# The first chunks of a perceiver block: who writes the warm-up's tile, and where the query work stands

## The chip, the cores and the metric

The kernel runs on one core of a Trainium2 chip. The metric is the device time of one execution in microseconds (us); lower is better. The engines are TensorE (PE; its weight loads are PEld), VectorE (DVE), ScalarE (ACT), GpSimd (POOL) and SyncE (SP), which here issues most of the DMA transfers. Each engine works through its own instructions in order, and semaphores order them among each other.

## The reference

x is 256 tokens of 512 values, the context is 4096 tokens of 512. Three residual steps follow each other. What this case touches is the first of them, cross-attention with 16 heads of 32:

```python
q = _qdq(x) @ _qdq(wq).T + bq          # x after layernorm
kv = cond @ wkv.T + bkv
k, v = jnp.split(kv, 2, axis=-1)
attn = jax.nn.softmax(jnp.einsum('bnhd,bmhd->bhnm', q, k) * scale, axis=-1)
o = jnp.einsum('bhnm,bmhd->bnhd', attn, v).reshape(B, N, C)
out = _qdq(o) @ _qdq(wp).T + bp
```

_qdq rounds to 8-bit steps with one scale for each token or each output channel. After it come a causal self-attention (16 query heads of 128, 4 key heads) and a feed-forward with silu(gate) * up, each after a layernorm and each added to x.

## The kernel before

The context is worked through in eight chunks of 512 tokens. For each chunk c PE computes four key blocks (`key_block`, 12 matmuls of 128x512 each: high and low parts of both operands, three passes over four slices) and four value tiles (12 matmuls each). ScalarE rounds the chunk's data to a high part (`high`, into h_ring), VectorE computes the low part (`low`, l_ring). ScalarE evacuates keys to kh_buf, VectorE computes their rest (`k_low`, kl_buf), and SyncE stores both to DRAM scratch, from where heads are loaded later into k_stack. Chunks 0 and 1 are written out; the rest run in a loop over pairs, the last pair written out again.

Chunk 0 is special: its data and the key weights come in four pieces, and PE works piece by piece (lines L1331 to L1337). Ahead of it, `keep_busy(7, 7)` issues seven fp32 matmuls of ident with itself (L1242), once GpSimd has written ones, ident and ident_b.

The query work is threaded into chunk 1. VectorE normalizes x, quantizes it to in_q (`quantize_tokens`), and quantizes wq and wp in halves (`quantize_weight_half`, nth 0 and 1 for wq, 2 and 3 for wp; each ends in w_q, L917, and counts w_used). Into these it threads `k_low` of chunk 1 and `low` of chunk 2. PE does `prepare_queries` between the keys and values of chunk 1: a row of token scales (ones times diag, L1262), the transposes of in_q (L396), then those of wq (L1254, after w_used 2). Ahead of value tile 3 it transposes wp; after tile 3, `project_queries` makes the row of wp's scales (L1280) and 16 projections (L1287). ScalarE copies the results to in_t, wq_t, wp_t (L662), sx_row and swp_row. VectorE then runs `split_queries`: high and low parts of the queries, which SyncE stores and loads again as q_max and q_stack (`load_q`). From chunk 2 on, PE threads first products of queries and keys (L1295) behind value tiles; they need q_max and k_stack.

The tile q_f lies in diag, k_stack[0] lies over the tiles of the query preparation, and bp_row over swp_row. PSUM has eight banks; `bank(i)` is one of them.

Of the kernel before, what the change touches and what calls it, by code (L numbers as in the profile page):

```python
# [109 lines left out]
def perceiver(nc, x_in, stream, wq_in, wp_in, bias_cols, bias_rows, out):  # L110
    with ExitStack() as ctx:
# [122 lines left out]
        q_f = diag[:, 0:NT, :].rearrange("p t n -> p (t n)")  # L234
# [18 lines left out]
        consts_ready = sem("consts_ready")  # L253
# [169 lines left out]
        def _(sp):  # L423
# [65 lines left out]
            sp.wait_ge(q_stored, 32 * KT)  # L489
            load_q(q_max[0], qm_loaded[0], 0)  # L490
# [65 lines left out]
        def _(pool):  # L556
# [12 lines left out]
            nc.gpsimd.memset(ones[:], 1.0).then_inc(consts_ready, 1)  # L569
# [7 lines left out]
            pool.wait_ge(ql_ready, KT)  # L577
            pool.wait_ge(ones_set, 1)
# [53 lines left out]
        def _(act):  # L632
# [32 lines left out]
            def context_chunk(i, k):  # L665
                c = 2 * i + k
                first, second = (isinstance(i, int) and c == n for n in range(2))
                if not first:
                    act.wait_ge(v_done, 4 * c)
                    high(act, c + 3, 1 - k, i + 1)  # L670
                for g in range(KT):
                    act.wait_ge(k_done, 4 * c + g + 1)
                    wait(act, k_stored[g], 32 * c)
                    nc.scalar.activation(kh_buf[:, g, :], key_bank(c, g), ACT.Identity,  # L674
                                         bias=biases[:, KT + g:KT + g + 1]).then_inc(kh_evac, 1)
                if first:
                    high(act, CTX0 + 1, 1, 1)
                if second:
                    act.wait_ge(row_done, 1)
                    nc.scalar.copy(sx_row[:], bank(5)[:, 0:N]).then_inc(row_evac, 1)  # L680
                    evacuate_tokens(0, in_t)
                    evacuate_transposed(3, (6, 7), wq_t)
                for mt in range(4):
                    if second and mt == 3:
                        evacuate_transposed(4, (4, 5), wp_t)
                    act.wait_ge(v_done, 4 * c + mt + 1)
                    nc.scalar.copy(v_all[:, :, 4 * c + mt, :],  # L687
                                   value_bank(c, mt).rearrange("p (h d) -> p h d", d=DH)).then_inc(v_evac, 1)
                if second:
                    act.wait_ge(row_done, 2)  # L690
                    nc.scalar.copy(swp_row[:], bank(6)).then_inc(row_evac, 1)

            context_chunk(0, 0)
            context_chunk(0, 1)
            with act.Fori(1, NCTX // 2) as i:
                context_chunk(i, 0)
                context_chunk(i, 1)
# [196 lines left out]
        def _(dve):  # L894
            order = Order(dve, dve_order)
            for kt in range(KT):
                dve.wait_ge(piece_loaded[kt], 32)
                nc.vector.tensor_copy(wkv_h[0][:, kt, :], wkv_raw[:, 0, kt, :]).then_inc(piece_wh, 1)
                dve.wait_ge(piece_wh, kt + 1)
                nc.vector.tensor_tensor(wkv_l[0][:, kt, :], wkv_raw[:, 0, kt, :], wkv_h[0][:, kt, :].bitcast(F32),  # L900
                                        ALU.subtract).then_inc(piece_l if kt < KT - 1 else l_ready, 1)
                wait_piece(dve, kt, piece_h, h_ready, 1)
                nc.vector.tensor_tensor(l_ring[0][:, kt, :], f_ring[0][:, kt, :], h_ring[0][:, kt, :].bitcast(F32),
                                        ALU.subtract).then_inc(piece_l if kt < KT - 1 else l_ready, 1)
# [15 lines left out]
            def token_row():  # L920
                dve.wait_ge(consts_ready, 3)
# [10 lines left out]
            def split_queries():  # L932
                dve.wait_ge(row_evac, 2)
                for g in range(KT):
# [3 lines left out]
                        out=q_f, in0=bank(7 if g < 2 else 4)[:, at], scalar=wq_s[:, g:g + 1], in1=sx_row[:],  # L938
# [30 lines left out]
            low(dve, CTX0 + 2, 0)  # L969
            quantize_weight_half(1, wq_s, between=lambda: k_low(1, 2))  # L970
            k_low(1, 3)
            for nth in (2, 3):
                quantize_weight_half(nth, wp_s)
# [261 lines left out]
        def _(pe):  # L1235
# [23 lines left out]
            def prepare_queries():  # L1259
# [4 lines left out]
                for t in range(NT):  # L1264
                    pe.wait_ge(quant_ready, t + 1)
                    transpose_tokens(t, in_q).then_inc(tr_done, 1)
                pe.wait_ge(w_used, 2)
                transpose_weights(0, (6, 7)).then_inc(tr_done, 1)

            def transpose_wp():  # L1270

                pe.wait_ge(w_used, 4)
                pe.wait_ge(tr_evac, 4)
# [3 lines left out]
            def project_queries():  # L1277

                pe.wait_ge(diag_ready, KT + NT)
                nc.tensor.matmul(bank(6), ones[:], diag[:].rearrange("p a n -> p (a n)"), start=True,  # L1280
                                 stop=True).then_inc(row_done, 1)
                for g in range(KT):
                    if g == 2:
                        pe.wait_ge(tr_evac, 6)
                    to = bank(7 if g < 2 else 4)[:, (g % 2) * N:(g % 2 + 1) * N]
# [3 lines left out]
                    if g % 2 == 1:  # L1289
                        last.then_inc(q_done, 1)  # L1290

# [25 lines left out]
            def context_chunk(i, k):  # L1317
# [35 lines left out]
                for mt in range(4):  # L1353
                    if second and mt == 3:
                        transpose_wp()
# [7 lines left out]
                    if k == 0 and not first:  # L1363
                        if mt == 0:
                            pe.wait_ge(qm_loaded[0], 48)
                            pe.wait_ge(k0_loaded, 48 * i)
                            pe.wait_ge(ql_ready, KT)

# [9 lines left out]
                if second:  # L1378
                    project_queries()

            pe.wait_ge(consts_ready, 3)
            keep_busy(7, 7)
# [404 lines left out]
```

## Time and profile before

| | |
|---|---|
| median of 3 runs | 617.87 us (616.87 to 618.75) |
| the profiled execution, its time | 621.24 us |
| its span, first to last instruction | 619.4 us |
| mean granted clock of TensorE | 0.994 |
| busy: PE, DVE, ACT, POOL | 597.2, 370.8, 302.9, 226.6 us |

A timeline row gives the start, the duration, the engine, the line of the kernel, the operation, the tile written and those read, the shapes and the count, and in brackets how long the engine sat idle before and what ended that. Matmuls are pipelined: the duration of one is longer than the distance to the next. A merged row (x16) has one duration from first start to last end.

### The profile page before, as it was taken

How to read it: one execution, taken by the hardware profiler on the slowest of the kernel's cores; microseconds unless marked ns; L12 is line 12 of the kernel's file. 1: busy time of each engine (PE TensorE's matmuls, PEld its weight loads, DVE VectorE, ACT ScalarE, POOL GpSimd, SP SyncE). 2: the span in 40 equal slices, each digit the busy share in tenths (PEclk: the TensorE clock that was granted, in tenths of full speed). 3: DMA queues.
4: the chain of work that ended last, by engine and by line, in shares of the span. 5: the costliest groups of instructions: out<-in, count | busy, mean ns of one | idle time of the engine just before them, and what ended most of it. 6: DMA issues, size and time to landing. Idle time of an engine off the chain costs nothing.

```text
span 619.4 us, 12489 instructions
## 1 busy us (share of the span) xinstructions
PE 597.2 (96%) x4386; PEld 478.7 (77%) x4386; DVE 370.8 (60%) x688; ACT 302.9 (49%) x437; POOL 226.6 (37%) x111
## 2 busy tenths in 40 slices
PE   8989999999999999999999999999799899999997
PEld 6867788888887667667777667775698789799996
DVE  4796622331434778787888788876754244376562
ACT  3444232333232666665566656555248668644441
POOL 0000200000002778888878888881001554410000
PEclk9999999999999999999999999999999899999999
DMA  8765456525629655566665556610041425245410
GB/s 292 277 215 167 164 181 195 176 95 162 210 95 274 185 155 152 149 159 164 163 158 148 148 153 167 161 57 2 1 146 58 138 72 200 69 181 194 174 63 34
DMA packets 29902, 92.19 MB, mean 149 GB/s; under 512 B 5488, under 2 KB 9584, under 8 KB 23280
## 3 DMA queue, kind: packets, MB, share of 16 engines
q1 hardware_dynamic: 28624, 89.67, 47.3%
q10 hardware_dynamic: 1248, 2.10, 0.9%
q8 instruction: 20, 0.33, 0.2%
q14 instruction: 10, 0.08, 0.0%
HBM read 65.02 MB, written 18.35 MB: 135 GB/s over the span
## 4 chain that ended last, share of the span: by engine, by line
PE 82%; DVE 9%; ACT 4%; issue 2%; POOL 2%; DMA 1%; SPq 0%; POOLq 0%; ACTq 0%; DVEq 0%
PE ps L341 15%; PE ps L342 14%; PE ps L343 14%; PE ps L1313 11%; PE ps L1420 9%; PE ps L1432 9%; PE ps L1446 4%; POOL p_sum L592 1%; PE ps L1409 1%; DVE kl_buf L950 1%; ACT h_ring L795 1%; DMA k_stack<-kh_scratch 1%; PE ps L1331 1%; DVE l_ring L314 1%; DMA f_ring<-stream 1%
## 5 line engine op out<-in xcount | busy, mean ns | idle before, releaser
L991 DVE TENSOR_REDUCE m_part<-ps 128x1 f32<-128x512 f32 x240 | 150.4, 683 | 39.4 <-PE ps L1313 39.1
L718 ACT ACTIVATE p_ring<-ps 128x1024 f32<-128x1024 f32 x128 | 125.8, 1023 | 80.0 <-PE ps L1420 44.2
L592 POOL TENSOR_TENSOR p_sum<-p_sum,p_ring 128x1024 f32<-128x1024 f32 x60 | 142.7, 2378 | 9.0 <-ACT p_ring L718 4.8
L1313 PE MATMUL ps<-k_stack,q_max 96*128 96x512 f32 x240 | 85.6, 427 | 1.5 <-issue 0.8
L1420 PE MATMUL ps<-q_stack,k_stack 98*128 98x256 f32 x512 | 80.7, 285 | 0.1
L1420 PEld LDWEIGHTS ps<-q_stack,k_stack 98*128 98x128 f32 x512 | 74.6, 189 | 6.8 <-ACT p_ring L718 1.7
L1432 PE MATMUL ps<-p_ring,v_head 128*32 128x256 f32 x1024 | 71.6, 383 | 0.1
L1313 PEld LDWEIGHTS ps<-k_stack,q_max 96*128 96x128 f32 x240 | 40.8, 188 | 26.4 <-issue 15.1
L950 DVE SCALAR_TENSOR_TENSOR kl_buf<-ps,biases,kh_buf 128x512 fp32r<-128x512 f32 x32 | 23.7, 749 | 58.2 <-ACT kh_buf L674 57.8
L314 DVE TENSOR_TENSOR l_ring<-f_ring,h_ring 128x2048 fp32r<-128x2048 f32 x22 | 50.2, 2288 | 12.5 <-ACT h_ring L310 12.5
L341 PE MATMUL ps<-xt_h,h_ring 128*128 128x256 f32 x200 | 56.8, 284 | 0.0
L343 PE MATMUL ps<-xt_h,l_ring 128*128 128x256 f32 x200 | 56.6, 283 | 0.0
L342 PE MATMUL ps<-xt_l,h_ring 128*128 128x256 f32 x200 | 56.6, 283 | 0.0
L687 ACT COPY v_all<-ps 128x512 f32 (+1 forms) x32 | 18.8, 588 | 68.2 <-PE ps L343 68.2
L592 POOL TENSOR_TENSOR p_sum<-p_ring 128x1024 f32<-128x1024 f32 x15 | 35.9, 2391 | 42.2 <-ACT p_ring L718 42.2
L1432 PEld LDWEIGHTS ps<-p_ring,v_head 128*32 128x32 f32 x1024 | 31.4, 109 | 25.2 <-issue 8.2
L341 PE MATMUL ps<-wkv_h,h_ring 128*128 128x512 f32 x128 | 50.9, 397 | 0.0
L342 PE MATMUL ps<-wkv_l,h_ring 128*128 128x512 f32 x128 | 50.4, 394 | 0.0
L343 PE MATMUL ps<-wkv_h,l_ring 128*128 128x512 f32 x128 | 50.4, 393 | 0.0
L310 ACT CAST h_ring<-f_ring 128x2048 fp32r<-128x2048 f32 x23 | 43.9, 1908 | 7.2 <-PE ps L343 7.2
L674 ACT ACTIVATE kh_buf<-ps,biases 128x512 fp32r<-128x512 f32 x32 | 21.7, 690 | 50.7 <-PE ps L343 47.8
L619 POOL TENSOR_TENSOR l_ring<-f_ring,h_ring 128x2048 fp32r<-128x2048 f32 x7 | 32.2, 4594 | 37.3 <-ACT h_ring L795 28.9
(197 smaller groups left out, 1087.8 us busy)
## 6 DMA issues: line engine op xcount, KB each, us to landing
f_ring<-stream SPq DMA_DIRECT2D x29, 1024.0 KB, 5.0
k_stack<-kh_scratch SPq DMA_DIRECT2D x60, 256.0 KB, 4.5
kh_scratch<-kh_buf SPq DMA_DIRECT2D x32, 256.0 KB, 4.8
kl_scratch<-kl_buf SPq DMA_DIRECT2D x32, 256.0 KB, 5.5
v_head<-v_all SPq DMA_DIRECT2D x16, 512.0 KB, 3.0
k_stack<-kl_scratch SPq DMA_DIRECT2D x30, 256.0 KB, 4.1
v_all<-stream SPq DMA_DIRECT2D x4, 256.0 KB, 4.7
f_ring<-stream SPq DMA_DIRECT2D x4, 256.0 KB, 5.7
```

Source lines behind the costliest of these rows:

```text
L310: nc.scalar.copy(h_ring[which][:], f_ring[which][:]).then_inc(h_ready, 1)
L314: nc.vector.tensor_tensor(l_ring[which][:], f_ring[which][:], h_ring[which][:].bitcast(F32), ALU.subtract).then_inc(l_ready, 1)
L341: nc.tensor.matmul(out_ap, lh, rh, start=start, stop=False)
L342: nc.tensor.matmul(out_ap, lh, rl, start=False, stop=False)
L343: return nc.tensor.matmul(out_ap, ll, rh, start=False, stop=stop)
L592: nc.gpsimd.tensor_tensor(p_sum[:, p, :], p_ring[:, 0, :] if n == 0 else p_sum[:, p, :], p_ring[:, c % 4, :], ALU.add).then_inc(sums_done, 1)
L619: nc.gpsimd.tensor_tensor(l_ring[w][:], f_ring[w][:], h_ring[w][:].bitcast(F32), ALU.subtract).then_inc(l_ready, 1)
L718: nc.scalar.activation(p_ring[:, c % 4, :], ps[:, 2 * (c % 2):2 * (c % 2) + 2, :].rearrange("p b n -> p (b n)"), ACT.Exp, scale=XSCALE).th ...
L991: nc.vector.reduce_max(m_part[:, j // NT, j % NT:j % NT + 1], maximum_bank(j), AX.X).then_inc(max_read, 1)
L1313: nc.tensor.matmul(maximum_bank(j), q_max[p][0:SPLIT_ROWS, at128(j % NT)], k_stack[p][0:SPLIT_ROWS, j // NT * D:(j // NT + 1) * D], start= ...
L1420: last = nc.tensor.matmul(ps[:, 2 * (c % 2) + k // 2, (k % 2) * N:(k % 2 + 1) * N], k_stack[p][0:SPLIT_ROWS + MAX_ROWS, at128(4 * c + k)], ...
L1432: last = nc.tensor.matmul(bank(7)[k * DH:(k + 1) * DH, 0:N], v_head[p][:, 4 * c + k, :], p_ring[:, c % 4, k * N:(k + 1) * N], start=c == 0 ...
```

## The change

VectorE writes ones at its start, with a semaphore of its own (ones_ready); PE warms up with eleven fp32 matmuls of ones with itself as soon as that is there, and waits for GpSimd's two ident tiles behind them. The transposes of wq move from ahead of value tile 0 of chunk 1 to ahead of value tile 1; those of wp move from ahead of tile 3 to behind the projections, which come right after tile 3; the row of wp's scales comes last, into bank 2. q_f moves into in_q, the queries' banks are 6 and 7. VectorE's low of chunk 2 moves behind the second half of wq and k_low(1, 3). ScalarE does high of chunk 3 at the end of chunk 1 rather than at the start of chunk 2, and its chunks 2 and 3 are written out. SyncE, GpSimd and PE wait for the second row copy (row_evac 2) ahead of their first use of what lies over the preparation's tiles.

```diff
--- before.py
+++ after.py
@@ -231,7 +231,7 @@
         wkv_raw = v_all[:].rearrange("p h m d -> p (h m d)")[:, 0:2 * KT * D].rearrange(
             "p (w k n) -> p w k n", w=2, k=KT)
         bp_row = swp_row
-        q_f = diag[:, 0:NT, :].rearrange("p t n -> p (t n)")
+        q_f = in_q[:].rearrange("p t d -> p (t d)").bitcast(F32)[:, 0:N]
 
         qh_buf = x_hat[:].rearrange("p t (g n) -> p (t g) n", n=N)
         ql_buf = o_all[:].rearrange("p t (g n) -> p (t g) n", n=N)
@@ -250,7 +250,7 @@
         x_loaded, rows_loaded, w_loaded = sem("x_loaded"), sem("rows_loaded"), [sem("w_loaded0"), sem("w_loaded1")]
         biases_loaded = sem("biases_loaded")
         w_used = sem("w_used")
-        consts_ready = sem("consts_ready")
+        consts_ready, ones_ready = sem("consts_ready"), sem("ones_ready")
         pool_order, dve_order = sem("pool_order"), sem("dve_order")
         dve_order_b, dve_order_c = sem("dve_order_b"), sem("dve_order_c")
         var_ready, rstd_ready = sem("var_ready"), sem("rstd_ready")
@@ -487,6 +487,7 @@
             context_chunk(0, 1)
             store_q()
             sp.wait_ge(q_stored, 32 * KT)
+            sp.wait_ge(row_evac, 2)
             load_q(q_max[0], qm_loaded[0], 0)
             load_q(q_stack[0], qs_loaded[0], 0)
             with sp.Fori(1, NCTX // 2 - 1) as i:
@@ -566,7 +567,6 @@
             order.step(nc.gpsimd.memset(minus_half[:], -0.5))
             for tile in (ident, ident_b):
                 order.step(nc.gpsimd.memset(tile[:], 0.0))
-            nc.gpsimd.memset(ones[:], 1.0).then_inc(consts_ready, 1)
             for tile in (ident, ident_b):
                 nc.gpsimd.affine_select(out=tile[:], in_=tile[:], compare_op=ALU.not_equal, fill=1.0, base=0,
                                         pattern=[[-1, P]], channel_multiplier=1).then_inc(consts_ready, 1)
@@ -575,6 +575,7 @@
 
 
             pool.wait_ge(ql_ready, KT)
+            pool.wait_ge(row_evac, 2)
             pool.wait_ge(ones_set, 1)
             nc.gpsimd.memset(k_stack[0][SPLIT_ROWS:P, :].bitcast(F32), 1.0).then_inc(ones_set, 1)
             pool.wait_ge(k_done, KT * NCTX)
@@ -664,8 +665,8 @@
 
             def context_chunk(i, k):
                 c = 2 * i + k
-                first, second = (isinstance(i, int) and c == n for n in range(2))
-                if not first:
+                first, second, third = (isinstance(i, int) and c == n for n in range(3))
+                if not first and not third:
                     act.wait_ge(v_done, 4 * c)
                     high(act, c + 3, 1 - k, i + 1)
                 for g in range(KT):
@@ -679,20 +680,22 @@
                     act.wait_ge(row_done, 1)
                     nc.scalar.copy(sx_row[:], bank(5)[:, 0:N]).then_inc(row_evac, 1)
                     evacuate_tokens(0, in_t)
-                    evacuate_transposed(3, (6, 7), wq_t)
                 for mt in range(4):
-                    if second and mt == 3:
-                        evacuate_transposed(4, (4, 5), wp_t)
+                    if second and mt == 1:
+                        evacuate_transposed(3, (6, 7), wq_t)
                     act.wait_ge(v_done, 4 * c + mt + 1)
                     nc.scalar.copy(v_all[:, :, 4 * c + mt, :],
                                    value_bank(c, mt).rearrange("p (h d) -> p h d", d=DH)).then_inc(v_evac, 1)
                 if second:
+                    high(act, CTX0 + 3, 1, 2)
+                    evacuate_transposed(4, (4, 5), wp_t)
                     act.wait_ge(row_done, 2)
-                    nc.scalar.copy(swp_row[:], bank(6)).then_inc(row_evac, 1)
-
-            context_chunk(0, 0)
-            context_chunk(0, 1)
-            with act.Fori(1, NCTX // 2) as i:
+                    nc.scalar.copy(swp_row[:], bank(2)).then_inc(row_evac, 1)
+
+            for i in range(2):
+                context_chunk(i, 0)
+                context_chunk(i, 1)
+            with act.Fori(2, NCTX // 2) as i:
                 context_chunk(i, 0)
                 context_chunk(i, 1)
 
@@ -893,6 +896,7 @@
         @block.vector
         def _(dve):
             order = Order(dve, dve_order)
+            nc.vector.memset(ones[:], 1.0).then_inc(ones_ready, 1)
             for kt in range(KT):
                 dve.wait_ge(piece_loaded[kt], 32)
                 nc.vector.tensor_copy(wkv_h[0][:, kt, :], wkv_raw[:, 0, kt, :]).then_inc(piece_wh, 1)
@@ -918,7 +922,7 @@
                 dve.wait_ge(w_used, nth + 1)
 
             def token_row():
-                dve.wait_ge(consts_ready, 3)
+                dve.wait_ge(consts_ready, 2)
                 for t in range(NT):
                     nc.vector.tensor_scalar(diag[:, t, :], ident[:], tok_s[:, t:t + 1], None,
                                             ALU.mult).then_inc(diag_ready, 1)
@@ -930,12 +934,12 @@
                                             ALU.mult).then_inc(diag_ready, 1)
 
             def split_queries():
-                dve.wait_ge(row_evac, 2)
+                dve.wait_ge(row_evac, 1)
                 for g in range(KT):
                     dve.wait_ge(q_done, g // 2 + 1)
                     at = slice((g % 2) * N, (g % 2 + 1) * N)
                     order.step(nc.vector.scalar_tensor_tensor(
-                        out=q_f, in0=bank(7 if g < 2 else 4)[:, at], scalar=wq_s[:, g:g + 1], in1=sx_row[:],
+                        out=q_f, in0=bank(6 + g // 2)[:, at], scalar=wq_s[:, g:g + 1], in1=sx_row[:],
                         op0=ALU.mult, op1=ALU.mult))
                     nc.vector.tensor_scalar(qh_buf[:, g, :].bitcast(F32R), q_f, biases[:, g:g + 1], None,
                                             ALU.add).then_inc(qh_ready, 1)
@@ -966,9 +970,9 @@
             quantize_weight_half(0, wq_s, between=lambda: k_low(1, 0))
             token_row()
             k_low(1, 1)
-            low(dve, CTX0 + 2, 0)
             quantize_weight_half(1, wq_s, between=lambda: k_low(1, 2))
             k_low(1, 3)
+            low(dve, CTX0 + 2, 0)
             for nth in (2, 3):
                 quantize_weight_half(nth, wp_s)
             dve.wait_ge(rows_loaded, 32)
@@ -1264,30 +1268,35 @@
                 for t in range(NT):
                     pe.wait_ge(quant_ready, t + 1)
                     transpose_tokens(t, in_q).then_inc(tr_done, 1)
+
+            def transpose_wq():
+
                 pe.wait_ge(w_used, 2)
                 transpose_weights(0, (6, 7)).then_inc(tr_done, 1)
 
             def transpose_wp():
 
                 pe.wait_ge(w_used, 4)
-                pe.wait_ge(tr_evac, 4)
                 pe.wait_ge(row_evac, 1)
                 transpose_weights(1, (4, 5)).then_inc(tr_done, 1)
 
             def project_queries():
 
-                pe.wait_ge(diag_ready, KT + NT)
-                nc.tensor.matmul(bank(6), ones[:], diag[:].rearrange("p a n -> p (a n)"), start=True,
-                                 stop=True).then_inc(row_done, 1)
+                pe.wait_ge(tr_evac, 4)
                 for g in range(KT):
-                    if g == 2:
-                        pe.wait_ge(tr_evac, 6)
-                    to = bank(7 if g < 2 else 4)[:, (g % 2) * N:(g % 2 + 1) * N]
+                    to = bank(6 + g // 2)[:, (g % 2) * N:(g % 2 + 1) * N]
                     for kt in range(KT):
                         last = nc.tensor.matmul(to, wq_t[:, kt, at128(g)], in_t[:, kt, :], start=kt == 0,
                                                 stop=kt == KT - 1)
                     if g % 2 == 1:
                         last.then_inc(q_done, 1)
+
+            def weight_row():
+
+                pe.wait_ge(v_evac, 7)
+                pe.wait_ge(diag_ready, KT + NT)
+                nc.tensor.matmul(bank(2), ones[:], diag[:].rearrange("p a n -> p (a n)"), start=True,
+                                 stop=True).then_inc(row_done, 1)
 
             def first_maximum_tile(j, k_at, read):
 
@@ -1351,8 +1360,10 @@
                     pe.wait_ge(v_evac, 4)
                     prepare_queries()
                 for mt in range(4):
-                    if second and mt == 3:
-                        transpose_wp()
+                    if second and mt == 1:
+                        transpose_wq()
+                    if k == 0 and not first and mt == 0:
+                        pe.wait_ge(row_evac, 2)
                     wait(pe, v_evac, 4 * c + mt - 1)
                     for kt in range(KT):
                         if first and mt == 0 and kt == KT // 2:
@@ -1365,6 +1376,7 @@
                             pe.wait_ge(qm_loaded[0], 48)
                             pe.wait_ge(k0_loaded, 48 * i)
                             pe.wait_ge(ql_ready, KT)
+                            pe.wait_ge(tr_evac, 6)
 
                         first_maximum_tile(mt, bass.ts(2 * i - 2 + mt // NT, D), 0 if mt < 2 else 4 * i - 5 + mt)
                     if last_one and mt in (1, 2):
@@ -1377,9 +1389,13 @@
                     pe.wait_ge(max_read, 4 * i)
                 if second:
                     project_queries()
-
-            pe.wait_ge(consts_ready, 3)
-            keep_busy(7, 7)
+                    transpose_wp()
+                    weight_row()
+
+            pe.wait_ge(ones_ready, 1)
+            for _ in range(11):
+                nc.tensor.matmul(bank(7)[:, 0:P], ones[:], ones[:], start=True, stop=True)
+            pe.wait_ge(consts_ready, 2)
             context_chunk(0, 0)
             context_chunk(0, 1)
             with nc.tensor.Fori(1, NCTX // 2 - 1) as i:
```

## Rows read from the trace of the kernel before

**Rows 1.** The page, part 1: busy us, share, instructions.
```profile
PE 597.2 (96%) x4386; PEld 478.7 (77%) x4386; DVE 370.8 (60%) x688; ACT 302.9 (49%) x437; POOL 226.6 (37%) x111
```

**Rows 2.** Windows, PE: stretch and length, busy (instructions), granted clock, DMA share, GB/s.
```profile
100.00:124.00 24.00, 24.00 (x108) 1.00 0.54 182
11.00:12.00 1.00, 1.00 (x4) 1.00 1.04 426
46.00:47.00 1.00, 1.00 (x6) 0.50 0.79 158
```

**Rows 3.** Timeline of PE, start: start us, us, what, count [idle before].
```profile
2.26 3.35 PE L1242 MATMUL ps<-ident 128*128 128x128 f32 x14 [2.26 <-POOL ident_b L571]
6.16 2.04 PE L1331 MATMUL ps<-h_ring,wkv_h 128*128 128x512 f32 x4 [0.55 <-ACT h_ring L635]
8.01 0.63 PE L1335 MATMUL ps<-h_ring,wkv_l 128*128 128x512 f32 x1
...
11.42 1.26 PE L1331 MATMUL ps<-h_ring,wkv_h 128*128 128x512 f32 x4
12.52 0.39 PE L1335 MATMUL ps<-h_ring,wkv_l 128*128 128x512 f32 x1
12.75 0.40 PE L1337 MATMUL ps<-l_ring,wkv_h 128*128 128x512 f32 x1
```

**Rows 4.** Timeline of PE, 45 to 77 us.
```profile
45.12 1.19 PE L1254 MATMUL ps<-ident_b,w_q 128*128 128x128 bf16 x16 [2.54 <-DVE w_q L917]
46.07 0.78 PE L341 MATMUL ps<-wkv_h,h_ring 128*128 128x512 f32 x1
...
49.73 0.40 PE L341 MATMUL ps<-wkv_h,h_ring 128*128 128x512 f32 x1
...
59.62 1.02 PE L1280 MATMUL ps<-diag,ones 128*128 128x512 f32 x2
60.48 1.91 PE L1287 MATMUL ps<-in_t,wq_t 128*128 128x256 bf16 x16
62.14 0.48 PE L341 MATMUL ps<-h_ring,wkv_h 128*128 128x512 f32 x1
...
68.35 0.50 PE L341 MATMUL ps<-h_ring,wkv_h 128*128 128x512 f32 x1 [0.49 <-DVE kl_buf L950]
...
76.65 0.40 PE L1295 MATMUL ps<-k_stack,q_max 96*128 x1
```

**Rows 5.** Timeline of VectorE (DVE), 14 to 67 us.
```profile
14.80 2.36 DVE L907 TENSOR_TENSOR wkv_l<-v_all,wkv_h 128x1024 fp32r<-128x1024 f32 x2 [2.13 <-ACT wkv_h L649]
19.50 2.73 DVE L950 SCALAR_TENSOR_TENSOR kl_buf<-ps,biases,kh_buf 128x512 fp32r<-128x512 f32 x4 [2.33 <-ACT kh_buf L674]
...
38.09 2.28 DVE L314 TENSOR_TENSOR l_ring<-f_ring,h_ring 128x2048 fp32r<-128x2048 f32 x1
...
44.37 0.69 DVE L917 TENSOR_SCALAR w_q<-w_raw 128x1024 bf16<-128x1024 f32 x1
...
55.53 0.87 DVE L929 TENSOR_SCALAR diag<-ident,wp_s 128x128 f32<-128x128 f32 x4
...
66.81 0.48 DVE L943 SCALAR_TENSOR_TENSOR o_all<-diag,biases,x_hat 128x256 fp32r<-128x256 f32 x1
```

**Rows 6.** Timeline of all engines, first 2 us.
```profile
0.75 1.28 ACT L635 ACT_TABLE_LOAD   x1 [0.75 <-PEq L1780]
...
1.42 0.20 POOL L569 MEMSET ones<- 128x128 f32 x1
```

**Rows 7.** DMA issues of 11.0 to 11.5 us: queue, count, KB, us to landing.
```profile
x_cur<-x_in ACTq DMA_DIRECT2D x1, 512.0 KB, 6.5
```

**Rows 8.** Timeline of ScalarE (ACT), near 57 us.
```profile
57.00 1.93 ACT L662 COPY wp_t<-ps 128x1024 bf16<-128x1024 bf16 x2 [0.32 <-PE ps L1254]
```

**Rows 9.** Timeline of SyncE's DMA queue (SPq), near 73 us.
```profile
73.41 0.32 SPq L462 DMA_DIRECT2D k_stack<-kh_scratch  x1
```

**Rows 10.** DMA issues of 72.0 to 73.8 us.
```profile
k_stack<-kl_scratch SPq DMA_DIRECT2D x1, 128.0 KB, 2.8
```

## The prediction

> **What bounds the kernel now.** I read the page first. TensorE (PE) is busy for 597.2 of the 619.4 us [rows 1], and the page's chain that ended last is mostly PE's. So a microsecond taken from PE ahead of the chunk loop ends in the total, if nothing else sets the pace of that loop. The windows of the steady chunks show PE busy for all 24.00 us of 24.00 [rows 2]: the loop is PE's own work, and what comes before it is shifted as a block. The change lies ahead of 62 us, so I read only that part closely.
>
> Next came PE's waits up to 70 us, where the one for w_q is the longest, and then PE's timeline, which shows three places where PE loses time.
>
> First place, the start. The warm-up runs from 2.26 us, after GpSimd's ident_b, to 5.61; the first real matmul starts at 6.16 [rows 3]. The eight 128x512 matmuls from 8.01 to 11.42 start 0.427 us apart. At 12.52 and 12.75 they are 0.23 us apart [rows 3]. The four matmuls between 11.42 and 12.52 take 1.10 us, which fits one at the old distance and three at the new, so PE's clock doubled at about 11.85 us. The column of the granted clock reads 1.00 here [rows 2]; it seems to hold nothing before its first change, and the distances decide: 1.2 GHz before, 2.4 GHz after.
>
> Second place, the query weights. PE finishes the tokens' transposes at 42.59 and waits 2.54 us for w_q, until 45.12 [rows 4]. Then the granted clock is down to 0.50 [rows 2]. From 46.07 to 49.73 there are nine distances, 3.66 us; at 0.227 us each they are 2.04; the later distances are short again from about 49.35. The fall costs 1.6 us on top of the wait.
>
> Third place, chunk 2. It starts at 62.14, and its third key block waits 0.49 us for kl_buf [rows 4]; with the restart, 0.88 us from matmul to matmul in place of 0.23, so 0.65 lost. VectorE was held by split_queries until 67.29 [rows 5].
>
> **Change, first part: the warm-up.** It removes GpSimd's memset of ones and PE's wait for three constants, and gives the memset to VectorE, which has nothing to do before the first piece of data. The engines' first instructions start at 0.75 [rows 6]. The trace has no VectorE memset. Bounds: 0.1 us (nothing but issue) and 0.5 us; GpSimd's memset of this very tile takes 0.20 [rows 6], which I take. PE starts at about 1.0 in place of 2.26. Seven fp32 matmuls are 14 records in 3.35 us, 0.21 apart but for the first, so eleven are 22 records, about 4.8 us, ending near 5.9 with the slow clock and earlier with the fast one. The first real matmul waits for h_ring's first piece as now, so it stays at 6.16; if the memset took 0.5 us, it would be late by about 0.1.
>
> What is gained is the moment at which the clock rises. The only other rise, at 49.35, came 4.2 us after PE resumed at 45.12 [rows 4]. The first came 5.7 us after the resumption at 6.16, and 9.6 after the first warm-up matmul. With PE running from 1.0 without the gap, 4.2 to 5.7 us give a rise at 5.2 to 6.7. Every matmul between the rise and 11.85 costs 0.227 in place of 0.427: with a rise at or before 6.16 that is 5.69 x 0.47 = 2.7 us, less some 0.1, an estimate, for l_ring's first piece, which PE then wants as soon as VectorE has it. With a rise at 6.7 it is 2.3. Supply should not take it back: the next piece is there when PE comes to it by the timeline of both engines, and ScalarE begins its next copy only after the last piece. Bounds: nothing (the rise stays where it is) and 2.6. I take 2.3.
>
> The Trainium skill's page "TensorE: Matmul & The Clock Gate", in Part 1 on the HAM clock gate, says that what watches PE's activity runs free of the kernel's start, so that the number of slow matmuls differs from run to run. The rows above are one execution and cannot show this. By that rule the first term would be a different one in each run, on either side of 2.3; by the rows it would be 2.3 each time. I use this for a rival below.
>
> Does the rest follow? VectorE's wkv_l halves end at 17.16 whatever PE does, and k_low(0, ...) starts at 19.50 now [rows 5]. So VectorE moves 2.34 us ahead, nearly as much as PE. x_cur, issued before 11.5 and 6.5 us on the way [rows 7], has landed by 18.0, ahead of its use at 19.8. f_ring's next chunk is wanted 2.3 us earlier as well; I assume it there, and its low has 2.4 us to spare. ScalarE's copies follow PE. The tightest place is k_low(1,0), due at 33.3, with PE's third key block of chunk 1 at 33.5: no wait, or 0.2.
>
> **Second part: wq behind value tile 0, low of chunk 2 behind k_low(1,3).** PE goes from the tokens' transposes (about 40.0) straight to value tile 0, 12 matmuls, 2.7 us, to 42.7. VectorE has w_q's second half at 45.06 now [rows 5]. It starts 2.34 earlier, and the 2.28 us of low(CTX0 + 2) no longer stand ahead of it [rows 5]: 40.5. So the transposes at 42.7 have 2.2 us to spare, the 2.54 us of waiting disappear, and with them the reason for the clock's fall. What covers the stall is the value tile; were it gone (the weights over 2.2 us late), each further microsecond would be on PE again. The low that is moved ends at 43.4 and is wanted by chunk 2 at 55: 12 us to spare. The load and the two pairs of K stores that SyncE holds behind it start near 43.4, ahead of today's, which come after w_q at 45.06. ScalarE's wq_t copies now stand between value copies 0 and 1; PE asks for copy 0 only at tile 2.
>
> The wait is worth 2.5. The fall is worth 1.6 in this execution, nothing in one where it does not happen. The three timed runs lie 1.9 us apart (616.87 to 618.75), as wide as this term, so I do not count it whole: 1.2.
>
> **Third part: queries ahead of wp's transposes, weight row last.** The same 16 projections (1.66 us), 16 transposes (0.95) and two records of the row (0.86) are issued [rows 4], in another order; nothing is saved on PE. VectorE's diag of wp_s ends at 56.40 now [rows 5], 54.06 after the shift. PE projects from about 52.0 to 53.6, transposes wp to 54.6 and then asks for diag: 0.5 us to spare. Chunk 2 starts at 55.5. split_queries no longer waits for swp_row, its 5.7 us run from 54.1 to 59.8, and k_low(2,0) is there at 60.6 or 60.8; PE wants it at 60.9. So the 0.65 us go, or all but 0.2. I take 0.6.
>
> ScalarE gets high(CTX0 + 3), 1.9 us, ahead of the wp_t copies, 1.93 [rows 8], and swp_row: 52.6 to about 57.2, with the first key block of chunk 2 ready at 58.3. Two more unrolled chunks on ScalarE add no work. SyncE's new wait for swp_row (57.2) stands ahead of load_q, and behind it are the K loads and chunk 2's K stores; it already waits there for q_stored, which comes after the last split at 59.8, so it costs nothing. GpSimd's k_stack memset likewise. PE's new waits ask for things long done.
>
> **The sum.** 2.3 + 2.5 + 1.2 + 0.6 = 6.6 us. Of this execution alone it would be 2.5 + 2.5 + 1.6 + 0.65 = 7.3: a span of 612.1 in place of 619.4, and a time of 613.9 in place of 621.24. The profiled time is 3.4 us above the median shown, so I take the sum from the median: 617.87 - 6.6 = 611.3.
>
> **Rivals.**
> (a) The clock decides otherwise: the rise does not come earlier, or not in most runs, and the fall was seldom there. Left are 2.5 + 0.6 and a part of the rest, 3.1 to 5: 612.9 to 614.8. For it: the rise in the start came late although PE had been at work since 2.26. Against: the gap from 5.61 to 6.16 goes. The skill's rule above points this way for single runs.
> (b) The stall moves: PE waits for wq or for diag, because VectorE, which works without a break up to 56.40, is later than the shift says. The slack at diag is 0.5 us; with 2 to 3 us late, 4 to 5 are left of the 6.6: 613 to 614.
> (c) The change comes to nothing: all of it is taken back before the loop ends, for instance by a fixed transfer. PE's 24.00 of 24.00 busy speaks against it. 617.9.
> (d) Slower: SyncE's wait for swp_row. Behind it stand load_q and load_k0. Today the last quarter of k_stack is issued at 73.41, 6.1 us after split_queries ends, and lands 2.8 us later at most, at 76.2 [rows 9, 10]; PE asks at 76.65 [rows 4], 14.5 us into chunk 2. In the new order that is 68.7 against 70.0, 1.3 us of slack, and swp_row comes 2.6 us ahead of the last split. So PE waits only when swp_row is over 3.9 us late, and past 3.9 + 6.6 = 10.5 us late the kernel is slower; 13 us late gives 620.4. Nothing in ScalarE's load speaks for it.
>
> **Chances.** Forecast, with its own range 609.3 to 612.8: 0.62. (a) 0.20, (b) 0.10, (c) 0.04, (d) 0.04. The range must leave out no more than 2 in 10: from 609.3 (both clock terms whole and the median run of before in the unlucky state) to 614.6. What can be told from no change is 0.3%, 1.9 us. Faster 0.92, same 0.04, slower 0.04.
>
> **What would show it.** PE's first matmul at about 1.0 us, waiting for VectorE; matmuls 0.23 apart from 6 or 7 us on; no wait for w_q, and no slice of granted clock under 1.00 near 45 us; wq's transposes at about 43, chunk 2's first matmul near 55.5; no wait for kl_buf in chunk 2. It would be wrong by the first term if the distances stay 0.427 until 10 us or later, by the second if PE stands before the wq transposes, and by the third if it stands before the weight row.

## The result, and the profile after

The changed kernel takes 614.99 us (median of five, 614.48 to 616.02), against 618.75 (616.87 to 619.93) for five runs of the kernel before. The ratio is 0.9946, interval 0.9925 to 0.9968: 3.3 us off, where I forecast 6.6 and a ratio of 0.9893. (The ratio compares fast executions alone, and is not the quotient of the two medians, 0.9939; of all executions below, the one of 856.25 us in run 10, at a mean granted clock of 0.635, is left out as slow.) The kernel is faster, and 0.4 us outside the range of 609.3 to 614.6. The median of before had been 617.87 over three runs; this makes 0.9 us of the miss of 3.7.

The profiled execution of the changed kernel has a span of 614.2 us and a time of 616.02, that is 5.2 us less than the profiled execution of before. The page, part 1, which answers to [rows 1]:

```profile
PE 596.1 (97%) x4394; PEld 478.5 (78%) x4394; DVE 370.9 (60%) x689; ACT 302.8 (49%) x437; POOL 226.4 (37%) x110
```

The timeline of PE in the first chunks, which answers to [rows 3, 4]:

```profile
1.06 5.06 PE L1397 MATMUL ps<-ones 128*128 128x128 f32 x22 [1.06 <-DVE ones L899]
5.89 1.45 PE L1340 MATMUL ps<-h_ring,wkv_h 128*128 128x512 f32 x4
7.18 0.39 PE L1344 MATMUL ps<-h_ring,wkv_l 128*128 128x512 f32 x1
7.40 0.39 PE L1346 MATMUL ps<-l_ring,wkv_h 128*128 128x512 f32 x1
```

```profile
42.62 1.07 PE L1258 MATMUL ps<-ident_b,w_q 128*128 128x128 bf16 x16
43.50 0.47 PE L341 MATMUL ps<-wkv_h,h_ring 128*128 128x512 f32 x1
...
51.79 1.92 PE L1289 MATMUL ps<-in_t,wq_t 128*128 128x256 bf16 x16
53.55 1.06 PE L1258 MATMUL ps<-ident_b,w_q 128*128 128x128 bf16 x16
54.44 1.08 PE L1298 MATMUL ps<-diag,ones 128*128 128x512 f32 x2
54.96 0.79 PE L341 MATMUL ps<-h_ring,wkv_h 128*128 128x512 f32 x1
```

The warm-up starts at 1.06, after VectorE's ones, and runs into the first real matmul without a gap. From 7.18 on the distances (from one start to the next) are 0.22 us. wq's transposes come at 42.62 without idle time (42.7 forecast). The projections, wp's transposes and the weight row follow each other, and chunk 2 starts at 54.96 (55.5 forecast). PE's waits of the first 100 us are now one row:

```profile
PE ps L1397 <- DVE ones L899: 1.1, 1, 1.1
```

VectorE has the second half of w_q at 40.26 (40.5), the weight row's diag at 53.82 (54.06), and its first k_low of chunk 2 at 60.41 (60.6). This answers to [rows 5]:

```profile
39.57 0.69 DVE L921 TENSOR_SCALAR w_q<-w_raw 128x1024 bf16<-128x1024 f32 x1
...
40.97 2.28 DVE L314 TENSOR_TENSOR l_ring<-f_ring,h_ring 128x2048 fp32r<-128x2048 f32 x1
...
52.94 0.88 DVE L933 TENSOR_SCALAR diag<-ident,wp_s 128x128 f32<-128x128 f32 x4
...
59.66 0.75 DVE L954 SCALAR_TENSOR_TENSOR kl_buf<-ps,biases,kh_buf 128x512 fp32r<-128x512 f32 x1 [0.26 <-DVE o_all L947]
```

ScalarE's copy to swp_row ends at 57.07, and SyncE goes on to load_q at 61.16. So up to chunk 2 every row stands within 0.6 us of where the prediction put it, and the two profiles are 7.7 us apart there (7.3 forecast for this pair): ScalarE's first value copy of chunk 2 is at 69.20, against 76.95. Where the other 2.5 us of this pair went, the windows of PE show (stretch and length, busy, granted clock, DMA share, GB/s):

```profile
44.00:45.00 1.00, 1.00 (x6) 1.00 1.00 156
428.00:429.00 1.00, 0.53 (x7) 1.00 0.00 0
429.00:430.00 1.00, 0.58 (x7) 0.87 0.00 0
430.00:431.00 1.00, 1.00 (x8) 0.50 0.08 16
431.00:432.00 1.00, 1.00 (x4) 0.50 0.00 0
432.00:433.00 1.00, 1.00 (x4) 0.50 0.00 0
433.00:434.00 1.00, 1.00 (x7) 0.92 0.00 0
```

The clock stays up near 45 us, as forecast, but falls from 1.00 to 0.50 at 429.7 (from here on, a fall), in a stage that the change doesn't touch: PE idles there, for 1.52 and 0.42 us, while VectorE quantizes the attention's output. In the profile of before the same two gaps bring no fall. It costs 1.5 us (from out_t's copy to xt_h's, 11.29 us against 9.78). The rest is 0.7 in the attention's heads and 0.3 at their beginning.

But 5.2 us is one pair of executions, and the medians are 3.8 apart. The question is thus which of the terms were the change's, and which belonged to the one execution of before that I had read.

### The profile page after: what moved, and what is told of

It is laid out like the page before. It is cut to its first block, busy times and chain, and to the rows that moved or that the text cites. A ratio compares the mean times of both kernels' runs of the same rounds, so it can differ in the third digit from the quotient of the medians.

```text
span 614.2 us, 12490 instructions
## 1 busy us (share of the span) xinstructions
PE 596.1 (97%) x4394; PEld 478.5 (78%) x4394; DVE 370.9 (60%) x689; ACT 302.8 (49%) x437; POOL 226.4 (37%) x110
## 4 chain that ended last, share of the span: by engine, by line
PE 88%; DVE 4%; ACT 3%; issue 2%; POOL 1%; DMA 1%; POOLq 0%; SPq 0%; ACTq 0%; DVEq 0%
PE ps L341 16%; PE ps L342 16%; PE ps L343 16%; PE ps L1322 11%; PE ps L1436 9%; PE ps L1448 9%; PE ps L1462 4%; POOL p_sum L593 1%; PE ps L1425 1%; ACT h_ring L798 1%; PE ps L1397 1%; DMA k_stack<-kh_scratch 1%; PE ps L1340 1%; PE ps L1304 1%; DVE p_sum L1075 1%
## 5 line engine op out<-in xcount | busy, mean ns | idle before, releaser
L341 PE MATMUL ps<-xt_h,h_ring 128*128 128x256 f32 x200 | 56.8, 284 | 0.0
L687 ACT COPY v_all<-ps 128x512 f32<-128x512 f32 (+1 forms) x32 | 18.8, 589 | 67.4 <-PE ps L343 67.4
L583 POOL MEMSET k_stack<- 32x4096 f32 x1 | 3.5, 3522 | 115.4 <-PE ps L343 115.4
```

The source lines that it names most:

```text
L341: nc.tensor.matmul(out_ap, lh, rh, start=start, stop=False)
```

## The experiments

Two theories stood at first. A: the front gives what its two profiles show, in every execution, and a fall that the change brings about behind it takes a part back. B: the clock decides anew in each execution, and the profile of before was an unlucky one, in its start or near 45 us. The kernels ran four at a time on one chip (1 to 4, 5 to 8, 9 to 12), each four beside their own runs of the kernel before (32, 18 and 34), and each ratio is against those.

**1. The kernel before, again.** No edit.

> The kernel before once more, to see which of its clock falls are its own. Theory A (the front gives its 7.5 us in every run, and a fall that the change makes near 430 us takes 1.3 back): this profile has its fall near 46 us again, chunk 2 starts at 62.1, ratio 1.000. Theory B (which gap of PE brings a fall is decided anew in each execution, so the fall near 46 us was in the profile of before and not in most timed runs): the slow stretches lie elsewhere, chunk 2 starts at 60.5 without one near 46, and the ratio is 1.000 with the single runs 1.5 us or more apart.

Ratio 0.9999 (0.9979 to 1.0018). Its profile has a span of 614.9 us, not 619.4. Chunk 2 starts at 58.24: theory B had 60.5, without the fall, and the other 2.3 us are the start. The start, PE's timeline:

```profile
2.26 3.36 PE L1242 MATMUL ps<-ident 128*128 128x128 f32 x14 [2.26 <-POOL ident_b L571]
5.79 1.71 PE L1331 MATMUL ps<-h_ring,wkv_h 128*128 128x512 f32 x4 [0.17 <-ACT h_ring L635]
7.34 0.39 PE L1335 MATMUL ps<-h_ring,wkv_l 128*128 128x512 f32 x1
7.57 0.39 PE L1337 MATMUL ps<-l_ring,wkv_h 128*128 128x512 f32 x1
```

With the old warm-up and with a gap, the distances are down to 0.23 at 7.34. The four matmuls ahead of it take 1.55 us, so the clock rose near 7.1 us, not at 11.85. (The kept trace also records the moment of the clock's changes: 6.99 us here, 11.79 in the profile of before.) The gap ahead of the first real matmul doesn't explain the late rise: in run 4 it is 0.50 us, against 0.55 there, and the clock rises at 7.28. PE waits 2.68 us for w_q here, and the windows show no fall:

```profile
41.00:42.00 1.00, 0.00 (x0) 1.00 0.04 8
42.00:43.00 1.00, 0.18 (x3) 1.00 0.00 0
43.00:44.00 1.00, 1.00 (x17) 1.00 0.07 20
44.00:45.00 1.00, 1.00 (x6) 1.00 1.00 336
```

So two of my four terms rested on something that another execution of the same kernel doesn't have.

**2. The warm-up alone.** The memset of ones and the eleven matmuls in the kernel before:

```diff
-            pe.wait_ge(consts_ready, 3)
-            keep_busy(7, 7)
+            pe.wait_ge(ones_ready, 1)
+            for _ in range(11):
+                nc.tensor.matmul(bank(7)[:, 0:P], ones[:], ones[:], start=True, stop=True)
+            pe.wait_ge(consts_ready, 2)
```

> The warm-up alone: ones by VectorE, eleven matmuls of it, nothing else changed. Theory A: chunk 2 starts 2.6 us earlier, 59.5 with the fall near 46 us, ratio 0.996. Theory B: chunk 2 starts 2.6 us earlier in a profile with an early rise; on average 1.5 to 2.3 us, ratio 0.9965.

Ratio 1.0003 (0.9982 to 1.0024): nothing, where the theories expected 0.996 and 0.9965. PE's start is earlier in the profile (first key copy at 15.63, against 16.22 in 1), and VectorE's w_q comes earlier with it (second half at 42.41, against 42.77). But the wait for w_q is still there, 2.75 us, and this time with a fall:

```profile
40.00:41.00 1.00, 0.00 (x0) 1.00 0.00 0
41.00:42.00 1.00, 0.00 (x0) 1.00 0.03 8
42.00:43.00 1.00, 0.54 (x6) 0.53 0.00 0
43.00:44.00 1.00, 1.00 (x12) 0.50 0.41 41
44.00:45.00 1.00, 1.00 (x6) 0.50 1.04 406
45.00:46.00 1.00, 1.00 (x5) 0.77 0.96 283
```

**3. The order alone.** The changed kernel with GpSimd's ones and `keep_busy(7, 7)` as before.

> The order alone: seven matmuls of ident as before, everything else as changed. Theory A: 4.7 us off, ratio 0.992, less 1.3 where a fall follows near 430 us. Theory B: the wait's 2.5 us and kl_buf's 0.65 are left, the fall's 1.6 only now and then: 3.2 us, ratio 0.995.

Ratio 0.9932 (0.9909 to 0.9955). The order has the whole gain, within the intervals. Theory B's 0.995 lies inside the interval, and so does A's 0.992.

**4. The old order with the wait filled**, by ten more matmuls of ident that nobody reads (a filler).

```diff
+                keep_busy(10, 7)
                 pe.wait_ge(w_used, 2)
                 transpose_weights(0, (6, 7)).then_inc(tr_done, 1)
```

> The kernel before with ten fp32 matmuls of ident (some 2.3 us) issued by PE where it waits for wq's second half; the wait itself stays. Both: no fall near 46 us. Theory A: ratio 0.9974 (1.6 us off). Theory B: the fall was in a part of the runs only, ratio 0.998 to 1.000.

Ratio 0.9978 (0.9960 to 0.9996). PE still waits for w_q, 0.3 us behind the filler, and the clock stays up. This is 1.4 us for the falls at this place, with an interval of 0.2 to 2.5, which holds the values of both theories; the profile can't say how often they come.

**5 and 6. The changed kernel and the order alone, on one chip.** No new edit.

> The changed kernel once more, beside the order alone on one chip. Theory C (what the runs so far suggest: the clock of the kernel before rises near 6 to 7 us too in most executions, so that the longer warm-up has little to give, and the order alone carries the gain): ratio 0.993 to 0.995, within 0.2% of the order alone; matmuls 0.23 apart from 6 to 7 us on. Rival D (the warm-up gives 1 us or more): ratio under 0.9915 and under that of the order alone.

> The order alone, with the warm-up of the kernel before, again. Theory C: ratio 0.9935 with its first look repeated, chunk 2 near 55 us. Rival D: 0.994 or more, 1 us or more above the changed kernel.

0.9944 (0.9927 to 0.9961) and 0.9958 (0.9941 to 0.9974). The changed kernel is 0.14% ahead here; in the first comparisons it was 0.14% behind. The two differences cancel. Rival D wanted under 0.9915 for the changed kernel, which its interval excludes; the 0.9 us between the two here comes near D's 1 us, but in the first comparisons the sign is the other way.

**7. No warm-up at all.**

```diff
             pe.wait_ge(ones_ready, 1)
-            for _ in range(11):
-                nc.tensor.matmul(bank(7)[:, 0:P], ones[:], ones[:], start=True, stop=True)
             pe.wait_ge(consts_ready, 2)
```

> The changed kernel with no warm-up matmul at all: what the warm-up is worth. PE then starts with its first real matmul near 5.2 us and the clock rises 4 to 6 us later, 9.5 to 11. That is 3 to 4.5 us of matmuls at 0.427 in place of 0.227, 1.4 to 2.1 us, if the rest follows; where VectorE's own start sets the pace of chunk 1, less: ratio 0.996 to 0.998. If it is as fast as the changed kernel, the start isn't on the path at all.

Ratio 1.0015 (0.9988 to 1.0041): 4.4 us slower than the changed kernel, more than expected. PE's timeline, start:

```profile
5.85 2.05 PE L1340 MATMUL ps<-h_ring,wkv_h 128*128 128x512 f32 x4 [5.85 <-ACT h_ring L636]
7.70 0.63 PE L1344 MATMUL ps<-h_ring,wkv_l 128*128 128x512 f32 x1
8.12 0.63 PE L1346 MATMUL ps<-l_ring,wkv_h 128*128 128x512 f32 x1
...
11.85 0.39 PE L1344 MATMUL ps<-h_ring,wkv_l 128*128 128x512 f32 x1
12.09 0.40 PE L1346 MATMUL ps<-l_ring,wkv_h 128*128 128x512 f32 x1
```

The clock rises near 10.7 us, and the first key copy is at 18.03, 2 us late, as worked out. The rest of this profile's loss is elsewhere: at the end of the chunk loop PE stands 2.40 us, with no releaser shown, and then the clock is down for over six more:

```profile
194.54 0.80 PE L1322 MATMUL ps<-k_stack,q_max 96*128 96x512 f32 x2 [2.40 <-issue]
```

```profile
194.00:195.00 1.00, 0.46 (x2) 1.00 0.98 218
195.00:196.00 1.00, 1.00 (x6) 0.50 1.04 221
196.00:197.00 1.00, 1.00 (x4) 0.50 1.00 201
200.00:201.00 1.00, 1.00 (x4) 0.50 0.16 50
```

So a warm-up is worth something; it is the step from seven matmuls that end at 5.6 us to eleven that end near 5.9 that gives little. What PE stands for at the loop's end is a load of k_stack, as shown further down; why PE is so far ahead of it here stays open.

**8. The changed kernel with a longer filler at the output's quantization**, where the fall at 429.7 was:

```diff
-                keep_busy(2 if t else 10, 3)
+                keep_busy(2 if t else 15, 3)
```

> The changed kernel with five more fp32 matmuls of ident (15 in place of 10) in PE's gap at the quantization of the attention's output, where the profile of the changed kernel has its fall at 430 us. Both theories: no slow stretch between 425 and 440 us, 0.5 us off on average (1.3 us in the executions that had the fall): ratio 0.992 to 0.994, slow stretch near 478 us unchanged.

Ratio 0.9927 (0.9909 to 0.9946), 1.0 us under the changed kernel beside it, though the two intervals overlap, and no fall there:

```profile
428.00:429.00 1.00, 0.60 (x8) 1.00 0.00 0
429.00:430.00 1.00, 0.58 (x8) 1.00 0.00 0
430.00:431.00 1.00, 0.95 (x9) 1.00 0.06 16
431.00:432.00 1.00, 1.00 (x7) 1.00 0.00 0
```

That alone doesn't show that the filler prevents a fall: of the nine profiles without it only that of the changed kernel has one at this place; the other eight, run 5 of the same kernel among them, have the same gaps of 1.52 and 0.42 us and none. The fall near 478 us, which this run was expected to keep, isn't in its profile either; eleven of the fourteen profiles have it.

**9 to 12. Both fillers, old and new warm-up, old and new order.** The edits of 4 and 8 in the kernel before (9) and in that with the new warm-up (10); the edit of 8 in the order alone (11) and in the changed kernel (12).

> Two fillers that keep PE at work in its waits, so that the clock falls of both places are out of the comparison: ten fp32 matmuls of ident in the wait for wq's second half, and 15 in place of 10 at the quantization of the attention's output. With the old warm-up and the old order. Theory C (a fall costs the same before and after; what moves the time is the order): 0.9978 of the filler at wq less 0.1 to 0.2% for the second, so 0.996 to 0.997. If the falls near 430 us belong to the changed kernel alone, the second filler gives nothing: 0.998.

> The same two fillers, the new warm-up, the old order. Theory C: the warm-up is worth the 0.3 to 0.6 us that the looks show at the first key copies (15.6 to 16.45 against 16.0 to 16.6 us), and less behind the wait for wq, whose end VectorE sets: within 0.1% of the kernel with the fillers and the old warm-up. Rival D (1 us or more): 0.2% under it.

> The old warm-up, the new order, the filler at the output's quantization (there is no wait for wq to fill). Theory C: the wait's 2.5 and kl_buf's 0.65 us under the old order with the fillers: 0.991 to 0.992. If the order is worth less than 2.5 us even so, something else behind it takes back.

> The changed kernel with the filler at the output's quantization, again: the fastest so far, 0.9927. Theory C: 0.992, within 0.1% of the new order with the old warm-up. Rival D: 0.2% under it.

| ratio (interval) | old order | new order |
|---|---|---|
| old warm-up | 0.9969 (0.9949 to 0.9989) | 0.9936 (0.9912 to 0.9960) |
| new warm-up | 0.9987 (0.9970 to 1.0004) | 0.9925 (0.9901 to 0.9950) |

The order is worth 0.33 and 0.62% here; the first is 2.0 us, less than the 2.5 that were set as the mark for something behind it that takes back. The warm-up costs 0.18% in one column and gives 0.11% in the other, within the intervals nothing.

**What all profiles say together.** Each profile dates the same four events: ScalarE's first key copy (how fast the start was), its first value copy of chunk 2, its last value copy, and its first copy to p_ring (the first head). The second column is the clock's rise as the trace records it; distances between matmuls gave 11.85, 7.1 and 10.7 for before, 1 and 7. In us:

| profile | rise | first key copy | to chunk 2 | chunk loop | to the first head |
|---|---|---|---|---|---|
| before | 11.79 | 18.69 | 58.26 | 121.01 | 3.14 |
| 1 before again | 6.99 | 16.22 | 56.82 | 121.01 | 2.65 |
| 2 warm-up alone | 4.51 | 15.63 | 58.46 | 121.01 | 2.69 |
| 4 before, one filler | 7.28 | 16.56 | 56.66 | 121.33 | 2.84 |
| 9 before, two fillers | 5.50 | 15.87 | 56.93 | 121.77 | 2.73 |
| 10 new warm-up, two fillers | 5.29 | 15.65 | 56.83 | 121.14 | 2.88 |
| changed | 6.49 | 16.07 | 53.13 | 121.11 | 3.43 |
| 5 changed again | 5.92 | 15.76 | 53.12 | 121.11 | 2.64 |
| 3 order alone | 6.61 | 15.97 | 53.13 | 121.11 | 2.86 |
| 6 order alone again | 7.39 | 16.28 | 53.13 | 121.11 | 3.56 |
| 8 changed, filler | 6.18 | 16.45 | 53.29 | 121.11 | 3.51 |
| 11 order alone, filler | 7.71 | 16.66 | 53.13 | 121.11 | 2.68 |
| 12 changed, filler again | 4.97 | 15.88 | 53.13 | 121.11 | 3.80 |
| 7 no warm-up | 10.69 | 18.03 | 53.13 | 121.11 | 6.06 |

The old warm-up has its first key copy at 15.87 to 16.66 in six profiles, mean 16.26, and at 18.69 in one, the profile that I read. The new one has it at 15.63 to 16.45 in six, mean 15.91. The rises are at 5.50 to 7.71 in the first six, mean 6.91, and at 4.51 to 6.49 in the other six, mean 5.56: the new warm-up does bring the rise 1.35 us forward, and 0.35 of it arrives at the first key copy. The stretch to chunk 2 is 56.7 to 56.9 in the old order without a fall, 58.3 and 58.5 with one, and 53.1 to 53.3 in the new, with no warm-up too: so a shift of the start passes on to chunk 2 in both orders. (In 4 and 9 the chunk loop takes 0.3 and 0.8 us longer than in 1; why, isn't shown.)

The timed runs list span and granted clock of each. Span times clock is the span without what falls cost, as far as PE has work all through them, since at half clock half of the time is then lost; the remainder is that cost. It is an estimate, and rather high: the fall at 429.7 would count 1.7 us and cost 1.5. The slow start isn't taken out by it, since the granted clock reads 1.00 there. Means:

| kernel | span | cost of falls | span without it |
|---|---|---|---|
| before (18 runs, beside 5 and 6) | 616.5 | 3.1 | 613.4 |
| 1 before again (12) | 616.4 | 3.0 | 613.3 |
| 2 warm-up alone (12) | 616.8 | 3.9 | 613.0 |
| 4 before, one filler (12) | 615.5 | 2.1 | 613.4 |
| 3 order alone (9) | 612.4 | 2.5 | 609.9 |
| 6 order alone again (7) | 613.0 | 2.6 | 610.3 |
| 5 changed again (6) | 612.1 | 2.1 | 610.0 |
| 8 changed, filler (6) | 611.3 | 1.4 | 609.9 |
| 7 no warm-up (12) | 617.4 | 4.6 | 612.7 |
| 9 before, two fillers (12) | 615.2 | 0.9 | 614.3 |
| 10 new warm-up, two fillers (11) | 615.7 | 1.4 | 614.3 |
| 11 order alone, filler (12) | 612.8 | 1.7 | 611.1 |
| 12 changed, filler (11) | 612.2 | 1.3 | 610.8 |

The standard error of a mean in the last column is 0.1 to 0.4 us, so that of a difference is 0.3 to 0.4. Run 7 is 5.3 us above 5: some 2.8 in the span without falls and 2.5 in falls. The filler at the output's quantization goes with fewer falls in all (1.4 against 2.1 in 8 and 5), but no run shows at which place.

## Why the prediction was wrong, step by step

**The warm-up, 2.3 us: the step that failed.** The mechanism ran as described: ones at 1.0, no gap, first real matmul at 5.9, an early rise. What was wrong is the other side of the difference. I took the rise at 11.85 for the kernel's, and it was this execution's; one in seven profiles with the old warm-up has it, and the same kernel has its rise at 6.99 in run 1. Between the other profiles the change is 0.35 us at the first key copy, and the span without falls is 0.4, 0.4, 0.0 and 0.2 us less in the four pairs with the same order (1 and 2, 6 and 5, 9 and 10, 11 and 12), 0.2 in the mean. The term measures 0.2 to 0.4, not 2.3. Why the clock rose so late in that one execution stays open. I had the warning in hand: the profiled execution was 3.4 us above the median of its own kernel, and 2.4 of these are this late rise (18.69 against 16.26 us at the first key copy). I scaled the sum to the median but left the term as that one execution gave it. The rule of the Trainium skill's page "TensorE: Matmul & The Clock Gate" (Part 1, on the HAM clock gate) that I cited, a different number of slow matmuls in each run, agrees with the profiles: 11.85 and near 7.1 us for one kernel. It stood in rival (a) at 0.20 when it belonged in the sum.

**The wait for w_q, 2.5 us, and kl_buf, 0.6 us: right.** The stretch to chunk 2 went from 56.8 to 53.1, 3.7 us where I had 3.1; the wait is 2.68 us in 1 and 2.75 in 2, where the start was earlier, because VectorE's w_q moves forward with PE's start nearly as far. In the span without falls the order is worth 3.4, 3.1 and 3.2 us (3 against 1, 6 against before, 11 against 9), which holds what the loop's end takes back (below). That it comes so close to 3.1 is in part luck: 0.6 more gained, some 0.4 given back, neither foreseen.

**The fall, 1.2 us: right in kind, too large.** The new order has none near 45 us. All falls together cost 3.0 to 3.1 us in the kernel before and 2.1 to 2.6 in the new order: 0.4 to 1.0 of the 1.2 is left. Part can be given back at other gaps, as at 429.7 in the profile after; with a filler there the falls cost 1.3 to 1.7 (8, 11 and 12).

**What else was given back.** Between the last value copy and the first head the new order takes 2.64 to 3.80 us in its seven profiles with a warm-up, mean 3.21, the old 2.65 to 3.14 in six, mean 2.82. The two ends of this range, 12 and then 5: SyncE's issue of the third of six loads of k_stack, its issue row (KB, us to landing), and PE's first row behind the loop:

```profile
181.78 0.51 SPq L455 DMA_DIRECT2D k_stack<-kh_scratch  x1
k_stack<-kh_scratch SPq DMA_DIRECT2D x1, 256.0 KB, 9.2
191.06 0.70 PE L1322 MATMUL ps<-k_stack,q_max 96*128 96x512 f32 x2 [1.06 <-issue]
```

```profile
181.15 0.53 SPq L455 DMA_DIRECT2D k_stack<-kh_scratch  x1
k_stack<-kh_scratch SPq DMA_DIRECT2D x1, 256.0 KB, 8.5
189.78 0.70 PE L1322 MATMUL ps<-k_stack,q_max 96*128 96x512 f32 x2
```

The row waits for the three loads of the second k_stack tile's first half, and the trace shows the last of these landing 0.09 us ahead of it in all fourteen profiles: this load ends the wait that the profile puts down to nothing. In the thirteen with a warm-up PE is ready for it 8.1 to 8.6 us after its issue, and it takes 8.4 to 9.4; PE loses 0.1 to 0.3 us where it takes up to 8.8, and 0.6 to 1.2 where it takes 9.0 or more. That is so in four of the seven profiles of the new order and in one of the six of the old. In 7 it takes 9.2 as well, but PE is ready 6.8 us after the issue and loses 2.6. Whether the new order makes the load slow, or these four are chance, no run shows: nothing here varied it.

**The rivals.** (a), the clock decides, at 612.9 to 614.8, is what happened in the main, for the warm-up far more than for the fall; its words "the rise does not come earlier" fit, not because the new rise was late but because the old one is early in most executions. The measured 614.99 is 0.2 above even its range, with a median of before 0.9 higher. (b) was not there: 2.4 us of slack at w_q and 0.6 at diag, as worked out. (c) is refuted by 3 and 5. (d) didn't happen either: swp_row came 2.3 us ahead of the last split, and no wait of PE in chunk 2 follows.

**The sum with measured terms**: 0.3 for the warm-up, 3.2 for the order and 0.7 for the falls are 4.2 us, against 3.3 (2.0 to 4.6) in the first comparison and 3.5 (2.4 to 4.5) in the second. From 618.75 that would be 614.6.

The lowest ratios are those of the changed kernel with the filler of 8: 0.9927 and 0.9925 in two comparisons, against 0.9944 to 0.9946 for the changed kernel. The intervals overlap, so that it is faster isn't shown.

## What to carry to other kernels

One profile is one draw of TensorE's clock. Before a slow stretch is entered into a sum, compare the profiled execution's time with the kernel's median; here 2.4 of the 3.4 us above it were a slow stretch that most other executions don't have. A second profile of the same kernel would have shown it. The wait for another engine's work was there each time (2.54, 2.68 and 2.75 us in the three profiles of the old order without a filler), so judge a change by such terms first. And an "issue" in brackets, with no releaser, can be the landing of a load: set the issue row's time to landing beside it.

## What the runs showed of the hardware that was not expected

The column of granted clock reads 1.00 from the start of a profile until its first fall, while the distances of 0.427 us ahead of the rise show half speed; the mean clock of a run so leaves the start out (run 6's profile has a mean of 1.000 and its rise at 7.39 us). The rise itself comes at 5.50 to 7.71 us in six profiles with one warm-up, and at 11.79 in a seventh. Idle time of the same length in the same place brings a fall in some executions and none in others: 2.68 us without (1), 2.75 and 2.54 with (2 and before). The gaps of 1.52 and 0.42 us at the output's quantization brought a fall in one of nine profiles. And loads of one size, 256 KB, from one place in the program, took 8.4 to 9.4 us to land, and where they took 9.0 or more PE stood 0.6 to 1.2 us for them (2.6 in 7).
